# Attention and mixture-of-experts layer: stack rows on every sixth partition, steps in twos

## The reference, cut to what matters

```python
q, k, v = (x @ W.T) / 16 per head            # W_query, W_key, W_value
scores = einsum('bhqd,bhkd->bhqk', q, k) / 4  # causal
out = einsum('bhqk,bhkd->bhqd', softmax(scores), v)
x = layernorm(x + (out @ W_proj.T) / 16)
# experts: softmax of x @ router_w.T, top 129 rows of each sequence,
# gelu(tokens @ w1 + b1) @ w2 + b2, times the gate, added at the rows
x = layernorm(x + experts(x))
```

## Time and profile before

| what | us |
|---|---|
| median of 3 runs | 906.53 (905.8 to 908.62) |
| profiled execution | 912.49 |
| its span, first to last instruction | 910.7 |
| start, up to the first `st` | 71 |
| sequences 1 to 4, each | 50.4 |
| sequence 7 | 47 |
| experts, from 477 | 434 |

### The profile page before, as it was taken

How to read it: one execution, slowest core, us unless ns; L and a number is a source line. 1 busy time by engine, 2 the same in 40 slices (tenths; PEclk the granted TensorE clock), 3 DMA queues, 4 the chain that set the end, 5 groups by cost and what they waited for, 6 DMA issues and landing times.

```text
span 910.7 us, 17163 instructions
## 1 busy us (share of the span) xinstructions
PE 818.5 (90%) x5876; PEld 612.6 (67%) x5876; DVE 601.3 (66%) x2059; ACT 533.2 (59%) x1048; POOL 472.5 (52%) x642
## 2 busy tenths in 40 slices
PE   4658999999999999997778999999999999999990
PEld 3434445454545445342348999999999999999990
DVE  4457787878877778898957854546464544636464
ACT  2225676758676766665748545546465656555554
POOL 6336575665556566333748446544444444435243
PEclk9778999999999999998899999999999999999995
DMA  4999686767686876910055223435243342523158
GB/s 139 167 142 180 104 153 104 146 122 150 121 155 116 153 129 120 217 53 25 22 193 169 36 30 59 96 80 139 45 94 75 55 125 44 143 31 58 20 142 262
DMA packets 89991, 100.52 MB, mean 110 GB/s; under 512 B 8625, under 2 KB 83377, under 8 KB 89777
## 3 DMA queue, kind: packets, MB, share of 16 engines
q1 hardware_dynamic: 72448, 77.92, 40.8%
q0 software_dynamic: 12800, 16.92, 11.5%
q10 hardware_dynamic: 4656, 4.59, 1.5%
HBM read 65.38 MB, written 33.62 MB: 109 GB/s over the span
## 4 chain that ended last, share of the span: by engine, by line
PE 70%; DVE 13%; ACT 6%; DMA 5%; issue 3%; SPq 2%; POOL 1%; ACTq 0%; POOLq 0%; DVEq 0%
PE y_ps L1358 21%; PE h_ps L1344 19%; PE av_ps L793 7%; PE st_ps L761 5%; DVE n_ps L625 5%; PE n_ps L776 4%; PE stage_ps L810 3%; PE stage_ps L818 3%; PE stage_ps L852 3%; DMA part_d<-w_raw 2%; PE tp_ps L1317 2%; ACT pt L523 1%; DVE nmax L625 1%; SPq L397 1%; PE stage_ps L843 1%
## 5 line engine op out<-in xcount | busy, mean ns | idle before, releaser
L625 DVE CUSTOM_DVE_ANT_0 n_ps<-n_ps,tri 128x512 f32<-128x512 f32 (+3 forms) x512 | 238.8, 519 | 85.3 <-PE n_ps L776 83.6
L523 ACT ACTIVATE pt<-st_ps 128x512 f32<-128x512 f32 x320 | 184.5, 602 | 64.7 <-PE st_ps L761 49.4
L1358 PE MATMUL y_ps<-w_parts,h_hi 128*128 128x256 f32 (+1 forms) x1152 | 215.2, 281 | 2.1 <-issue 1.5
L1178 ACT ACTIVATE g<-h_ps,b 128x384 f32<-128x384 f32 (+1 forms) x192 | 104.1, 542 | 162.2 <-PE h_ps L1344 144.1
L1358 PEld LDWEIGHTS y_ps<-w_parts,h_hi 128*128 128x128 f32 (+1 forms) x1152 | 172.5, 177 | 6.0 <-issue 1.8
L1150 POOL DMA_INDIRECT acc<-y,tok_no x64 | 103.1, 1611 | 139.7 <-DVE y L1293 130.0
L1344 PE MATMUL h_ps<-tt_hi,w_parts 128*128 128x384 f32 (+1 forms) x768 | 169.7, 323 | 3.7 <-issue 2.0
L1279 DVE TENSOR_TENSOR h_lo<-g,h_hi 128x384 fp32r<-128x384 f32 (+1 forms) x176 | 90.4, 514 | 118.4 <-ACT h_hi L1183 98.2
L452 POOL TENSOR_SCALAR_AFFINE_SELECT pt<-pt 128x256 f32<-128x256 f32 (+1 forms) x320 | 109.9, 361 | 108.7 <-ACT pt L523 108.0
L1358 PE MATMUL y_ps<-w_parts,h_lo 128*128 128x256 f32 (+1 forms) x576 | 161.5, 280 | 0.0
L761 PE MATMUL st_ps<-w_parts 99*128 99x512 bf16 (+3 forms) x512 | 126.1, 308 | 16.8 <-ACT pt L523 14.6
(11 more groups left out here) (192 smaller groups left out, 1075.7 us busy)
## 6 DMA issues: line engine op xcount, KB each, us to landing
w_parts<-part_d SPq DMA_DIRECT2D x192, 128.0 KB, 6.3
w_raw<-in_w SPq DMA_DIRECT2D x16, 1024.0 KB
part_d<-w_raw SPq DMA_DIRECT2D x96, 128.0 KB, 6.3
w_raw<-in_xt SPq DMA_DIRECT2D x8, 512.0 KB, 5.3
res<-in_x SPq DMA_DIRECT2D x8, 512.0 KB, 11.4
x<-res SPq DMA_DIRECT2D x8, 512.0 KB, 3.2
acc<-res SPq DMA_DIRECT2D x8, 512.0 KB, 5.2
fin<-acc SPq DMA_DIRECT2D x4, 512.0 KB, 3.9
```

The source lines that it names most:

```text
L523: nc.scalar.activation(pt[:, slot % PT_RING, n % UP, :], st_ps[at % ST_RING][:, :], ACT.Exp, scale=S_SCALE).then_inc(exp_done, 1)
L625: ins = nc.vector.tensor_tensor_reduce(out=src[:, h, :], in0=src[:, h, :], in1=mask, scale=-1.0, scalar=-BIG_NEG, op0=ALU.add, op1=ALU.min ...
L1178: nc.scalar.activation(g[:, at % G_RING, 0:cols], h_ps[at % H_RING][:, 0:cols], ACT.Gelu, bias=b1[:, e, n:n + 1]).then_inc(g_done, 1)
L1358: ins = nc.tensor.matmul(y_ps[at % Y_RING][0:rows, 0:C], x[:, q % 2, m, toks], w[e % 2][:, m, :], start=i == 0, stop=i == len(terms) - 1)
```

## The change

Two things are changed. Row d of block `at` of a stack lies on partition 6 d + at and no longer on 16 at + d, for q and k alike; the 96 rows hold the same values in another order. And the places go in twos: at an even place come `st` and `nat` of this and of the next place, then the `av` sets of both, then the stages of this place, then those of the next.

```diff
@@ -117,14 +117,16 @@
                 if (i, g, k) == (-1, 3, 0):
                     yield "nmcut", 0, 0
                     yield "nm", 0, 0
-                if 0 <= i < B:
-                    yield "st", i, (2 * g) * UP + k
-                if 0 <= nat_b < B:
-                    for n in range(N_QUARTER * k // 10, N_QUARTER * (k + 1) // 10):
-                        yield "nat", nat_b, nat_0 + n
                 group = i * GROUPS + g - 1
-                if k in AV_PLACES and 0 <= group < B * GROUPS:
-                    yield "av", group, AV_PLACES.index(k)
+                for at in (k, k + 1) if k % 2 == 0 else ():
+                    if 0 <= i < B:
+                        yield "st", i, (2 * g) * UP + at
+                    if 0 <= nat_b < B:
+                        for n in range(N_QUARTER * at // 10, N_QUARTER * (at + 1) // 10):
+                            yield "nat", nat_b, nat_0 + n
+                for at in (k, k + 1) if k % 2 == 0 else ():
+                    if at in AV_PLACES and 0 <= group < B * GROUPS:
+                        yield "av", group, AV_PLACES.index(at)
@@ -394,7 +396,7 @@
                 for which, stack, blocks in ((0, qst, Q_PARTS), (1, kst, K_PARTS)):
                     for at, part in enumerate(blocks):
                         src = part_d[which, b % 2, part, n, :, :].rearrange("(h d) n -> d h n", d=D)
-                        sp.dma_start(stack[at * D:(at + 1) * D, b % 2, HH * n:HH * (n + 1), :], src).then_inc(stack_in[n][b % 2], 16)
+                        sp.dma_start(stack[at:KQ:len(blocks), b % 2, HH * n:HH * (n + 1), :], src).then_inc(stack_in[n][b % 2], 16)
```

## The result

The change makes the kernel slower. The ratio is 1.0087, with a 95% interval from 1.0058 to 1.0117. The prediction was 898.2 us, with a range from 888 to 905, faster.

What follows compares the result with a forecast made beforehand. TensorE was taken to set the pace in the sequences, while the start waited on DMA transfers. From 912.49 us profiled, −10.2 (stack rows) and +1.9 (twos) gave 904.2, or 898.2 against the median of 906.53; range 888 to 905.

Steps and rivals of the forecast that it cites:

- The stack rows: In the start, loads spread over 96 partitions land sooner and the first `st` comes 10.65 us earlier; −10.2 us in all.
- the start of `nmcut`: In the start, `nmcut` was to begin at 52 to 54 us, taken as 53, instead of 62.91.
- bound by the issue: Spread stack loads were to go one every 0.46 us, the last landing some 2 us behind its issue.
- the end at −7: Small end of the stack rows' gain: `nmcut` at 55 us and half a clock in `qk`.
- estimate of 0.6 us for a load: From the Trainium skill's port table, for a stack load whose rows lie six partitions apart.
- Quarter 0: Twos save 0.37 us and lose about 0.15, since `nat` 3 meets VectorE still at the units of place 9; −0.2 us.
- Quarter 1: `nat` 15, pulled ahead of `av`, makes TensorE stand until `nmcut` and unit 12 are through; +0.8 us, from 0.3 to 1.3.
- the rival's "against": In quarter 1, GpSimd's second operation starts 1.2 us after the first, so not all of both can fall on `nmcut`'s casts.
- Quarter 2: No wait replaces the saved entries, and `proj` in twos no longer meets VectorE; −0.8 us, from −0.4 to −1.0.
- Quarter 3: ScalarE's chain from the maxima's copy starts after both `av` sets, so the next `st` comes 0.5 us later, at most 1.0.
- slower: `nat` 15 behind `nmcut`: Rival: the pull-ahead costs 2 us in quarter 1, likewise 0.6 in quarter 3; 910.3 us at 2 us a sequence; chance 0.06.
- The saving itself: Two `av` sets side by side leave out one entry and exit, 0.18 us; 0.37 a quarter, 1.5 a sequence.

Runs made afterwards that it cites:

- e1: New stack rows kept, steps single as before the change (first hunk undone); ratio to the kernel before 0.9917.
- e5: Single steps and new stack rows, with the `av` sets written in pairs in all quarters; ratio to the kernel before 0.9895.
- e10: Changed kernel plus eight matmuls with unread results ahead of `nat` 15 in quarter 1; ratio to the kernel before 1.0009.
- e4: Changed kernel with the two casts of `nmcut` written as reduces over an axis of one element; ratio to the kernel before 0.9961.
- e11: Changed kernel with `nmcut`'s two casts as one-element reduces and its two subtractions as scalar_tensor_tensor; ratio to the kernel before 0.9946.
- e8: Changed kernel with places 4 and 5 written apart as before in both quarter 1 and quarter 3; ratio to the kernel before 0.9891.
- e3: Changed kernel with places 4 and 5 of quarter 1 alone written apart as before; ratio to the kernel before 0.9963.
- e6: Changed kernel with `nat` 15 of quarter 1 moved behind the two sets of `av`; ratio to the kernel before 0.9936.
- e9: Single steps and new stack rows, `av` sets in pairs in quarters 0 to 2 only; ratio to the kernel before 0.9753, median 889.8 us.
- e12: Changed kernel with `nat` 15 behind both `av` sets in quarter 1 and places 4 and 5 of quarter 3 apart; ratio to the kernel before 0.9805.
- e2: Steps in twos kept, stack rows as before the change (second hunk undone); ratio to the kernel before 1.0157, 924.7 us.

## Why the prediction was wrong

**The stack rows: right in mechanism, 2.7 us too much.** Predicted −10.2 with ends of −7 and −11.5; e1 measures −7.5 us (−5.7 to −9.3). Landings are at 2.4 to 4.2 us, predicted 2 to 3.5; the DMA share of a sequence is 0.45, as predicted; `nat` 0 starts at 34.25 in e1, predicted 34.7; the first `st` came at 61.5 in the changed kernel and 63.6 in e1, predicted 59 to 62. The term that was off is the start of `nmcut`, taken at 53: 53.57 and 55.93. Two things make it late. The loads were to be "bound by the issue" at 0.46 us each, and each takes 0.65 us (7.76 us for twelve). So the second twelve hold SyncE until 42.0, the last store behind them lands 3.5 us after its issue where 1.9 was priced, and ScalarE takes the tile that frees the bank for the second `v` at 48.21 in e1 (48.08 in the changed kernel), predicted 46.4. SyncE and ScalarE of e1:

```profile
34.35 7.65 SPq L397 DMA_DIRECT2D w_parts<-part_d  x12
48.21 0.60 ACT L554 ACTIVATE w_raw<-stage_ps 128x512 bf16<-128x512 f32 x1 [0.38 <-DMA part_d<-w_raw]
```

The rest is the clock from 50 us on, which the end at −7 had named for `qk` and which came at `v`: with it `nmcut` starts at 55.93, without it, in e5, at 53.55. The prediction's estimate of 0.6 us for a load, from the Trainium skill's port table ("SBUF — State Buffer"), was on a load's transfer; what sets the pace at nearly that value is SyncE's issue, and no run shows the transfer alone.

**Quarter 0, predicted −0.2, measured −0.3** (9.56 us for 9.83).

**Quarter 1, predicted +0.8 with ends of +0.3 and +1.3, measured +1.1 or +2.5 to +2.7.** The place, the releaser and the wait were right: `nmcut` started 3.7 us into the quarter and ended 6.3 us in, the late end of the range; the wait, predicted at 1.3 to 2.3 us, is 2.13. (The wait at `nm` before, which the prediction has at 0.48 us, is 0.34 by its row in sequence 3.) The step that failed is the one that ended there. It took the cost of TensorE's wait to be its length. In three sequences of five, and in sequence 6 too, the clock is at 1.2 GHz behind the wait, and the same `av`, `nm` and `ot` take 1.1 us more, to the end of the quarter 1.4 to 1.6. e10 shows that this is from idling and weighs it, 0.78% or about 7 us. The prediction had the clock's fall in the start before its eyes (0.82) and did not ask where else a wait of 2 us would lead. The Trainium skill, "TensorE: Matmul & The Clock Gate", part 1, puts the rule the right way round for this: a slow clock is the default and activity lifts it. e10 against the changed kernel agrees.

Beside it stands a smaller step that failed, in the rival's "against": that not all of GpSimd's two operations can fall on the casts. Nearly all can. `nmcut` has four operations in a row, and when the first starts 0.07 us behind GpSimd's it takes 0.95 us more, is let go in the gap of 0.07 us, and the third meets the next and takes 0.84 us more. e4 and e11 show that it isn't a matter of which of the four: with the casts exempt, the subtractions wait, and `nmcut` takes 2.36 us instead of 2.63.

**Quarter 2, predicted −0.8 (−0.4 to −1.0), measured −0.4.** The entries and exits are saved, but `nat` 25 waits 0.27 us for VectorE ahead of the pair.

**Quarter 3, predicted +0.5, at most 1.0, measured +0.7.** The reason was right: the copy of the maxima and `split` come one set later. e8 takes it out. What it can leave behind was missed again: the half clock in the next quarter 0, in four sequences of five in e3 and two in e6 (behind a wait of 1.4 us at `st`), in three in e5 (no wait over 0.8 us), and in one each in e4, e10 and e11. In e8, e9 and e12, where ScalarE's chain starts early, it is in none. Nor is it in the changed kernel, behind the same 1.4 us.

**The sum.** Predicted +0.3 us in a sequence, 1.9 us in all. Without the clock the measured quarters add up to +1.1; with it sequences 1 to 5 of the two profiles are 1.9 us longer on the mean, and the ratios give 2.2 (15.4 us in seven). So this part was 13.5 us short, about half of it the clock, beside 2.7 us from the stack rows. The prediction's rival "slower: `nat` 15 behind `nmcut`", priced at 910.3 us from 2 us in a sequence, is what happened, at a chance of 0.06. It was held back by an argument on VectorE and GpSimd that stood on no row, and it lacked the clock. Its point of decision was 1.5 us in a sequence; with the 7.5 us that the stack rows really give it is 1.1, and 2.2 lies beyond either.

**The saving itself** was under-, not over-estimated: 1.5 us in a sequence for eight pairs, and e9 saves 2.3 with six, though 0.4 of that is the wait at `nm` that vanished. In quarter 0, with no wait in play, two pairs save 0.47 us (9.83 to 9.36), predicted 0.37: in e9 the sets of 512 and 384 columns last 1.53 us together (219.67 to 221.20), where they took 0.88 + 0.78 = 1.66, and with one entry of 0.09 that is 0.22 us a pair and not 0.18.

## What to carry to other kernels

A step that is pulled ahead of a long block takes that block away as the cover of somebody's chain. Before such a move, look which engine's chain the pulled step waits for, and leave it behind the block; here one step decides between 0.87% slower and 0.64% faster. Price a new wait on TensorE as its length and then, as the bad case, the work behind it at half the clock (behind the wait of 2.1 us it came in three sequences of five, and in four in e2; behind that of 1.4 us in four of five in e3 and in none in the changed kernel), and look for it in the stretch that follows too. Give a gain on the bottleneck engine only where the row of waits shows that it is the bottleneck: pairs in three quarters of four beat pairs in all.

## What the runs showed of the hardware

- Eight idle-filling matmuls in a sequence, whose result nobody reads, make the kernel 0.78% faster (1.0009 against 1.0087): the granted clock of quarter 1 stays at 1.00 where it fell to 0.66 over 4.5 us.
- The wait alone doesn't decide whether the clock falls: the same wait of 2.13 us left it full in sequences 1 and 2 and halved it in 3 to 5. Nor does it take a wait of that length: in e5 no wait is over 0.8 us, and quarter 0 has the half clock in three sequences of five. What tells these apart no run here shows.
- VectorE's 0.18 us casts take up to 1.13 us and its 0.19 us subtractions up to 0.98 us, until GpSimd's running operation ends; a reduce over one element does the same rounding in 0.17 to 0.19 us beside it.
- DMA loads onto every sixth partition land in 2.7 us where those onto sixteen neighbours took 3.0 to 8.8 us in a row of twelve, at equal bytes; but SyncE issues each in 0.65 us instead of 0.46.
